# Two more units of an adjacency matrix by DMA transpose, earlier loads and shifted column sums in a two-layer graph kernel

## The chip, the cores and the metric

The kernel runs on one core of a Trainium2 chip. The time is device time in microseconds (us) of one execution; lower is better. PE is TensorE, DVE is VectorE, ACT is ScalarE, POOL is GpSimd and SP is the queue that issues the DMAs.

## What is computed

`x` is 2048x512 and `adj` is 2048x2048, a symmetric pattern of nonzeros with values that are not symmetric. All arithmetic of the reference is float32.

```python
h = jnp.maximum(_layernorm(x, axis=-1), 0.0)
# first layer: quantised features and weights, then a product with adj
weight_q = _weight_quant((weight - mean) / std, wgt_alpha, 3)
support = jnp.matmul(_act_quant(h, act_alpha, 4) / act_delta, weight_q / wgt_delta)
support = jax.nn.relu(support * act_delta * wgt_delta)
support_q = _act_quant(support, act_alpha2, 4)
x = x + jnp.matmul(adj / s, support_q / support_delta) * s * support_delta
# second layer: a normalised symmetric adjacency, and two products
h = jnp.maximum(_layernorm(x, axis=-1), 0.0)
a = (adj + adj.T) * 0.5 + jnp.eye(2048)
deg = jnp.sum(a, axis=1)
dinv = jnp.where(deg > 0, deg ** (-0.5), 0.0)
x = x + (adj @ (dinv[:, None] * a * dinv[None, :])) @ h
```

The second layer is worked as `adj @ (A @ h)`, so there are three products with a 2048x2048 matrix: the first layer's, one with the normalised symmetric matrix (called the second product below) and one with `adj` again.

## The kernel before

`adj` is cut into 32 units: unit u is the block of 128 rows number u // 2, and of these rows the columns of half u % 2 (128 x 1024 float32, 512 KB). A product with `adj` on PE needs the blocks transposed, as a pair of float16 parts (a high part, scaled by 256, and a low part that holds the rest). Both parts of all units stay in the tile `at` for the whole kernel. A unit gets there in one of two ways.

- A turned unit: PE transposes it in float32, eight blocks of 128x128 (`turn`, line 1067), ACT writes the high part from PSUM (`hi_turned`, line 514) and takes the row sum (`row_sum`, line 481), DVE takes the column sums of its eight blocks (`column_sum`, line 743) and writes the low part (`lo_turned`, line 754).
- A moved unit (the list `MOVED`): ACT writes the high part before the transpose and takes the row sum with it (`hi_rows`, line 504), DVE writes the low part (`lo_rows`, line 759), both into one of three staging places, and SP issues one DMA transpose of both parts into `at` (`move`, line 335). The k-th moved unit can be staged when the (k-3)-th has landed. PE has no work with it. For the odd units the column sums come from an accumulator that POOL adds up in float32 (line 463) and that PE turns once, as the unit called "acc". For the even moved units (`EVEN`) ACT sums the columns of the transposed unit, half a unit at a time (`sum_blocks`, line 490, four blocks each), in the places that `SUMS_OF` gives.

Each engine's order is written out by hand. PE: for each row block r from 0 to 15 `layer0(r, ...)` (line 1083), 32 matmuls of 128x512 that add up the first layer's product in PSUM; ahead of it, or in gaps of it, the turns in `TURNS[r]`. `layer0(r)` needs unit 2r at its start and unit 2r+1 at its second chunk, and, since PSUM has two banks for it, the features of block r-2 out of the bank: it waits for `x1_ready` at r-1, which `x1_tile(r - 2)` on DVE signals.

DVE (loop of line 945): in stage r, `x1_tile(r - 1)` (line 876: one SCALAR_TENSOR_TENSOR of line 882, then the statistics of lines 884 and 885), the turned unit of the stage, `lo_rows` of the units in `MOVES[r]`, the columns of units 0 and 2 (`column_sum_late`, line 749), and in four stages a part of the second product's preparation: `sum_unit(v)` (line 921) adds both parts of `at` across to a fresh copy of `adj`, `sum_lo(v)` (line 936) splits off the low part of that sum. ACT has `sum_hi(v)` (line 579) between the two.

SP (line 312): loads (`rows`, `rows_again`) and transposes (`move`) stand in one order in one queue, and a load into a used slot waits until the unit before it is done. `LOADS` says which loads follow which move. POOL adds unit u of the odd ones when it has arrived and `layer0` of an early enough block is done (`ADD_AT`).

The loop of DVE's stages, in which the order matters:

```python
for r in range(1, 14):
    x1_tile(r - 1)
    ...
    for u in moves[1:]:
        lo_rows(u)
    if r - 3 in LATE_SUMS:
        column_sum_late(r - 3)
    ...
    if r == 10:
        sum_unit(1)
```

Of the kernel before, what the change touches and what calls it, by code (L numbers as in the profile page):

```python
# [9 lines left out]
T = N // P  # L10
KD = D // P
W = N // 2
B = W // P
# [4 lines left out]
AHEAD = 20  # L18
# [8 lines left out]
EVEN = (10, 12, 14, 18, 20, 22, 26)  # L27
# [6 lines left out]
def gnn_kernel(nc, x, adj, adj_scale, weight, wgt_alpha, act_alpha, act_alpha2, out):  # L34
# [5 lines left out]
    with ctx:  # L40
# [242 lines left out]
        for u in EVEN:  # L283
# [6 lines left out]
        MOVES = {1: [9], 2: [10, 11], 3: [12], 4: [13, 14], 5: [15], 6: [17, 18], 7: [19, 20], 8: [21, 22],  # L290
                 9: [23, 25], 10: [26], 11: [27, 29]}
# [5 lines left out]
        SUMS_OF = {5: [[(10, FIRST)], [], [(10, LAST)]], 7: [[(12, FIRST)], [(12, LAST)], []],  # L297
                   8: [[(14, FIRST)], [(14, LAST)], []], 9: [[(18, FIRST)], [(18, LAST)], []],
                   10: [[], [], [(20, FIRST)]], 11: [[], [(20, LAST)], [(22, FIRST)]],
                   12: [[], [], [(22, LAST), (26, FIRST)]], 13: [[], [], [(26, LAST)]]}  # L300
# [12 lines left out]
        def _(sp):  # L313
# [47 lines left out]
            for u in range(2, 12):  # L361
# [6 lines left out]
            move(3)  # L368
            move(5)
            sp.wait_ge(sq_ready, T // 2)  # L370
            rows(14)
            rows(15)
            move(7)
            LOADS = {9: [16], 10: [17], 11: [18], 12: [19], 13: [20], 14: [21], 15: [22], 17: [23], 20: [24], 21: [25], 22: [26],
                     23: [27], 25: [29, 28], 26: [30], 27: [31]}
            for r in range(1, 12):
                for u in MOVES[r]:
                    move(u)
                    for w in LOADS.get(u, []):
                        if w < AHEAD:  # L380
                            rows(w)
                        else:
                            rows_again(w)
# [82 lines left out]
        def _(act):  # L466
# [156 lines left out]
            for r in range(1, 14):  # L623
                moves = MOVES.get(r, [])
                ahead, between, behind = SUMS_OF.get(r, [[], [], []])
                for u in TURNS[r][:1]:
                    turn_hi(u)
                for u, blocks in ahead:
                    sum_blocks(u, blocks)
                for u in moves[:1]:  # L630
                    hi_rows(u)
                for u in TURNS[r][:1]:
                    sum_rows(u)
                for u in TURNS[r][1:]:
                    turn_hi(u)
                    sum_rows(u)
                for u, blocks in between:
                    sum_blocks(u, blocks)
                for u in moves[1:]:
                    hi_rows(u)  # L640
                for u, blocks in behind:
                    sum_blocks(u, blocks)
                if r == 9:
                    sum_hi(0)
                if r == 11:
                    sum_hi(1)
# [22 lines left out]
        def _(dve):  # L669
# [275 lines left out]
            for r in range(1, 14):  # L945
# [11 lines left out]
                if r - 3 in LATE_SUMS:  # L957
                    column_sum_late(r - 3)
                if r == 8:
                    sum_unit(0)  # L960
                if r == 9:
                    sum_lo(0)
                if r == 10:
                    sum_unit(1)
                if r == 11:
                    sum_lo(1)

            a, b = LATE_SUMS[0] * B, (LATE_SUMS[-1] + 1) * B
            link(nc.vector.memset(pause[:, :], 0.0))
            link(nc.vector.tensor_scalar(colp[:, a:b], colp[:, a:b], 1.0 / SA, None, ALU.mult))  # L970
# [5 lines left out]
            for moved_sums in (rs3[:, ADDED[1] // 2:ADDED[-1] // 2 + 1, 1],  # L976
                               rs3[:, 5:14:2, 0], rs3[:, 6:11:4, 0]):
                last = nc.vector.tensor_scalar(moved_sums, moved_sums, 1.0 / SA, None, ALU.mult)
# [268 lines left out]
```

## Time and profile before

| | before |
|---|---|
| median of 3 runs | 494.21 us |
| lowest and highest | 493.84 and 494.96 us |
| the profiled execution | 493.84 us |
| its span in the trace | 492.0 us |
| PE busy | 97% of the span |
| DVE busy | 55% |
| ACT busy | 31% |
| POOL busy | 10% |

The span is the time between the first and the last instruction of the trace; some 1.8 us of the execution's time lie around it. Start times below count from the span's start. The stages r = 1 to 13 of the first product run from 45 to 143 us, `layer0(14)` and `layer0(15)` to 157 us, the second product to 323 us, and the third to the end. The number behind a waiting instruction, in square brackets, is how long its engine was idle ahead of it and what ended that.

### The profile page before, as it was taken

How to read it: one execution, taken by the hardware profiler on the slowest of the kernel's cores; microseconds unless marked ns; L12 is line 12 of the kernel's file. 1: busy time of each engine (PE TensorE's matmuls, PEld its weight loads, DVE VectorE, ACT ScalarE, POOL GpSimd, SP SyncE). 2: the span in 40 equal slices, each digit the busy share in tenths (PEclk: the TensorE clock that was granted, in tenths of full speed). 3: DMA queues.
4: the chain of work that ended last, by engine and by line, in shares of the span. 5: the costliest groups of instructions: out<-in, count | busy, mean ns of one | idle time of the engine just before them, and what ended most of it. 6: DMA issues, size and time to landing. Idle time of an engine off the chain costs nothing.

```text
span 492.0 us, 6358 instructions
## 1 busy us (share of the span) xinstructions
PE 478.2 (97%) x2358; PEld 232.0 (47%) x2358; DVE 268.4 (55%) x360; ACT 154.5 (31%) x300; POOL 47.3 (10%) x54
## 2 busy tenths in 40 slices
PE   2899999999999999999999999999999999999997
PEld 2655444444544444444444444444444444444446
DVE  5967997779998788876997777240100001000010
ACT  1887834867651354353521211230000000000000
POOL 2321953223100000000000000000000000000000
PEclk9999999999999999999999999999999999999999
DMA  8986999999794332323232321054000000100001
GB/s 303 403 319 161 224 218 248 215 233 255 178 302 191 89 126 87 125 87 99 85 117 93 121 85 43 0 183 180 36 29 21 21 21 21 43 21 21 21 23 43
DMA packets 62507, 62.65 MB, mean 127 GB/s; under 512 B 45464, under 2 KB 45720, under 8 KB 62488
## 3 DMA queue, kind: packets, MB, share of 16 engines
q1 hardware_dynamic: 62480, 62.40, 43.5%
q8 instruction: 11, 0.18, 0.1%
q14 instruction: 8, 0.07, 0.1%
q10 hardware_dynamic: 8, 0.00, 0.0%
HBM read 42.99 MB, written 8.39 MB: 104 GB/s over the span
## 4 chain that ended last, share of the span: by engine, by line
PE 92%; DVE 3%; DMA 2%; ACT 1%; SPq 1%; issue 1%; POOL 0%; ACTq 0%
PE ps_a L1202 32%; PE ps_p L1100 20%; PE ps_p L1165 8%; PE ps_a L1165 7%; PE ps_b L1165 7%; PE ps_h L1165 4%; PE ps_m L1165 4%; DMA feat<-in_x 2%; PE ps_b L1051 1%; PE ps_h L1100 1%; PE ps_m L1100 1%; DVE small L942 1%; PE ps_b L1218 1%; PE ps_a L1218 1%; PE ps_a L1051 1%; PE ps_a L1079 1%
## 5 line engine op out<-in xcount | busy, mean ns | idle before, releaser
L1100 PE MATMUL ps_p<-small,at 128*128 128x512 f16 x448 | 99.1, 379 | 0.0
L1020 DVE SCALAR_TENSOR_TENSOR feat<-ps_a,feat 128x512 f32<-128x512 f32 (+1 forms) x16 | 10.8, 675 | 148.7 <-PE ps_a L1202 144.2
L1202 PE MATMUL ps_a<-small,at 128*128 128x512 f16 x360 | 80.1, 379 | 0.0
L1202 PE MATMUL ps_a<-a_in,at 128*128 128x512 f16 x360 | 80.1, 379 | 0.0
L1100 PEld LDWEIGHTS ps_p<-small,at 128*128 128x128 f16 x448 | 43.7, 98 | 50.2
L585 ACT ACTIVATE split<-a_in 128x1024 f16<-128x1024 f32 x30 | 31.7, 1057 | 101.8 <-PE ps_p L1165 90.0
L938 DVE TENSOR_TENSOR split<-a_in,split 128x1024 f16<-128x1024 f32 x30 | 36.7, 1224 | 34.1 <-ACT split L585 34.1
L1202 PEld LDWEIGHTS ps_a<-small,at 128*128 (+1 forms) x360 | 35.2, 98 | 42.5
L1202 PEld LDWEIGHTS ps_a<-a_in,at 128*128 (+1 forms) x360 | 35.2, 98 | 42.5
L1165 PE MATMUL ps_p<-feat,split 128*128 (+1 forms) x180 | 43.9, 379 | 0.5 <-DVE small L942 0.5
L1165 PE MATMUL ps_a<-feat,split 128*128 (+1 forms) x180 | 43.8, 379 | 0.0
L1165 PE MATMUL ps_b<-feat,split 128*128 (+1 forms) x180 | 43.8, 379 | 0.0
L929 DVE TENSOR_TENSOR a_in<-a_in,at 128x1024 f32<-128x1024 f32 x30 | 36.7, 1225 | 1.0
L928 DVE SCALAR_TENSOR_TENSOR a_in<-a_in,at 128x1024 f32<-128x1024 f32 x30 | 36.5, 1217 | 0.0
L1165 PEld LDWEIGHTS ps_p<-feat,split 128*128 128x128 f16 x180 | 17.5, 98 | 22.0 <-DVE small L942 1.0
L1165 PEld LDWEIGHTS ps_a<-feat,split 128*128 128x128 f16 x180 | 17.6, 98 | 21.4 <-issue 0.5
L1165 PEld LDWEIGHTS ps_b<-feat,split 128*128 128x128 f16 x180 | 17.6, 98 | 21.2
L1165 PE MATMUL ps_h<-feat,split 128*128 (+1 forms) x90 | 24.3, 379 | 0.0
L1165 PE MATMUL ps_m<-feat,split 128*128 (+1 forms) x90 | 24.3, 379 | 0.0
L463 POOL TENSOR_TENSOR at<-at 128x1024 f32<-128x1024 f32 x8 | 21.4, 2672 | 12.6 <-PE ps_p L1100 11.8
L761 DVE SCALAR_TENSOR_TENSOR at<-at 128x1024 f16<-128x1024 f32 x12 | 18.9, 1599 | 0.0
L463 POOL TENSOR_TENSOR at<-at,a_in 128x1024 f32<-128x1024 f32 x6 | 15.9, 2654 | 26.8 <-DMA a_in<-in_adj 16.7
(182 smaller groups left out, 436.2 us busy)
## 6 DMA issues: line engine op xcount, KB each, us to landing
a_in<-in_adj SPq DMA_DIRECT2D x46, 512.0 KB, 3.9
at<-in_adj SPq DMA_DIRECT2D x16, 512.0 KB, 8.6
out<-feat SPq DMA_DIRECT2D x31, 256.0 KB, 4.2
feat<-in_x SPq DMA_DIRECT2D x8, 512.0 KB, 11.1
feat<-out SPq DMA_DIRECT2D x4, 1024.0 KB, 9.4
at<-in_L_gnn_weight SPq DMA_DIRECT2D x2, 512.0 KB, 3.9
split<-in_adj SPq DMA_DIRECT2D x1, 512.0 KB, 16.3
tmp<-in_adj SPq DMA_DIRECT2D x1, 512.0 KB, 16.4
```

What stands on the lines that cost most here:

```text
L463: nc.gpsimd.tensor_tensor(acc, acc, unit_in(u), ALU.add).then_inc(acc_done, 1)
L585: nc.scalar.activation(part(v % 2, 0), sum_in(v), ACT.Copy).then_inc(shi, 1)
L761: nc.vector.scalar_tensor_tensor(stage(u, 1), unit_in(u), SA, stage(u, 0), ALU.mult, ALU.subtract)\
L928: link(nc.vector.scalar_tensor_tensor(u3, u3, SA, at_across(h, 0, j), ALU.mult, ALU.add))
L929: last = nc.vector.tensor_tensor(u3, u3, at_across(h, 1, j), ALU.add)
L938: nc.vector.tensor_tensor(part(v % 2, 1), sum_in(v), part(v % 2, 0), ALU.subtract).then_inc(slo, 1)
L1020: nc.vector.scalar_tensor_tensor(out, products, 1.0 / (SA * SZ), out, ALU.mult, ALU.add).then_inc(y_out, 1)
L1051: last = nc.tensor.matmul(sup_banks(m)[:, t * D:(t + 1) * D], hT[m % 2][:, (t * KD + k) * P:(t * KD + k + 1) * P], w_int[:, k * D:(k + 1) ...
L1100: last = nc.tensor.matmul(l0_bank(r), at_block(r, lo, j), small[:, j * D:(j + 1) * D], start=(j == 0 and lo == 0), stop=(j == T - 1 and lo ...
L1165: last = nc.tensor.matmul(BANK[t], part(k, lo)[:, t * P:(t + 1) * P], g_part(j, g_lo), start=(first and lo + g_lo == 0), stop=False)
L1202: last = nc.tensor.matmul(BANK[n], at_block(t, lo, j), z_part(j, z_lo), start=(j == 0 and lo + z_lo == 0), stop=(j == T - 1 and lo == 1))
L1218: last = nc.tensor.matmul(BANK[1 + h][:, 0:DH], at_block(T - 1, lo, j), z_part(j, z_lo)[:, h * DH:(h + 1) * DH], start=(j == 0 and lo + z_ ...
```

## The change

Units 16 and 24 join `EVEN`, so they are moved and no longer turned; there are then 23 moved units and 9 turned ones. SP issues the loads of units 14 to 19 together, between the moves of 3 and 5 and behind a wait for the first layer's features, where two of them stood after the move of 5 and four stood after the moves of 9 to 12. The columns of 10, 14 and 18 are summed on DVE by `column_sum_late`, in stages 5, 7 and 9, and no longer on ACT; ACT's other sums have new places. `sum_unit(1)` goes from DVE's stage 10 to the end of stage 9, `sum_lo(1)` from stage 11 to stage 10, and ACT's `sum_hi(0)` and `sum_hi(1)` stand ahead of `hi_rows` in stages 9 and 10, where they stood at the ends of stages 9 and 11.

```diff
@@ -24,7 +24,8 @@
 GROUPS = (0, 2, 4, 8, 12, T)
 LATE_GROUPS = (0, 13, T)
 LATE_SUMS = (0, 2)
-EVEN = (10, 12, 14, 18, 20, 22, 26)
+EVEN = (10, 12, 14, 16, 18, 20, 22, 24, 26)
+SUMMED_LATE = (10, 14, 18)
 MOVED = tuple(sorted(tuple(range(3, 30, 2)) + EVEN))
 ADDED = tuple(range(1, 30, 2))
 TURNED = tuple(u for u in range(UNITS) if u not in MOVED)
@@ -287,17 +288,16 @@
         ROW_SUMS = {2: [0], 4: [1, 2, 4], "acc": []}
 
 
-        MOVES = {1: [9], 2: [10, 11], 3: [12], 4: [13, 14], 5: [15], 6: [17, 18], 7: [19, 20], 8: [21, 22],
-                 9: [23, 25], 10: [26], 11: [27, 29]}
+        MOVES = {1: [9], 2: [10, 11], 3: [12], 4: [13, 14], 5: [15, 16], 6: [17, 18], 7: [19, 20], 8: [21, 22],
+                 9: [23, 24, 25], 10: [26], 11: [27, 29]}
         ADD_AT = {u: (u - 7) // 2 for u in ADDED if u >= 9}
 
 
 
         FIRST, LAST = range(0, B // 2), range(B // 2, B)
-        SUMS_OF = {5: [[(10, FIRST)], [], [(10, LAST)]], 7: [[(12, FIRST)], [(12, LAST)], []],
-                   8: [[(14, FIRST)], [(14, LAST)], []], 9: [[(18, FIRST)], [(18, LAST)], []],
-                   10: [[], [], [(20, FIRST)]], 11: [[], [(20, LAST)], [(22, FIRST)]],
-                   12: [[], [], [(22, LAST), (26, FIRST)]], 13: [[], [], [(26, LAST)]]}
+        SUMS_OF = {6: [[(12, FIRST)], [(12, LAST)], []], 8: [[(16, FIRST)], [(16, LAST)], []],
+                   10: [[(20, FIRST)], [], [(20, LAST), (22, FIRST)]], 11: [[(22, LAST)], [], [(24, FIRST)]],
+                   12: [[], [], [(24, LAST), (26, FIRST)]], 13: [[], [], [(26, LAST)]]}
         PARTS = sum(len(place) for places in SUMS_OF.values() for place in places)
 
         def wait_moved(engine, u):
@@ -366,21 +366,18 @@
             rows(12)
             rows(13)
             move(3)
+            sp.wait_ge(sq_ready, T // 2)
+            for u in range(14, AHEAD):
+                rows(u)
             move(5)
-            sp.wait_ge(sq_ready, T // 2)
-            rows(14)
-            rows(15)
             move(7)
-            LOADS = {9: [16], 10: [17], 11: [18], 12: [19], 13: [20], 14: [21], 15: [22], 17: [23], 20: [24], 21: [25], 22: [26],
-                     23: [27], 25: [29, 28], 26: [30], 27: [31]}
+            LOADS = {13: [20], 14: [21], 15: [22], 16: [23], 20: [24], 21: [25], 22: [26], 23: [27], 24: [28], 25: [29],
+                     26: [30], 27: [31]}
             for r in range(1, 12):
                 for u in MOVES[r]:
                     move(u)
                     for w in LOADS.get(u, []):
-                        if w < AHEAD:
-                            rows(w)
-                        else:
-                            rows_again(w)
+                        rows_again(w)
             for v in range(2, 6):
                 free_slot(UNITS - 6 + v)
                 sums(v)
@@ -627,6 +624,8 @@
                     turn_hi(u)
                 for u, blocks in ahead:
                     sum_blocks(u, blocks)
+                if r in (9, 10):
+                    sum_hi(r - 9)
                 for u in moves[:1]:
                     hi_rows(u)
                 for u in TURNS[r][:1]:
@@ -640,10 +639,6 @@
                     hi_rows(u)
                 for u, blocks in behind:
                     sum_blocks(u, blocks)
-                if r == 9:
-                    sum_hi(0)
-                if r == 11:
-                    sum_hi(1)
 
             late_sqrt(0)
             g_tile(0)
@@ -956,17 +951,22 @@
                     lo_rows(u)
                 if r - 3 in LATE_SUMS:
                     column_sum_late(r - 3)
+                for k, u in enumerate(SUMMED_LATE):
+                    if r == (5, 7, 9)[k]:
+                        wait_moved(dve, u)
+                        column_sum_late(u)
                 if r == 8:
                     sum_unit(0)
                 if r == 9:
                     sum_lo(0)
+                    sum_unit(1)
                 if r == 10:
-                    sum_unit(1)
-                if r == 11:
                     sum_lo(1)
 
             a, b = LATE_SUMS[0] * B, (LATE_SUMS[-1] + 1) * B
             link(nc.vector.memset(pause[:, :], 0.0))
+            late_sums = colp[:, :].rearrange("p (u b) -> p u b", b=B)[:, SUMMED_LATE[0]:SUMMED_LATE[-1] + 1:4, :]
+            nc.vector.tensor_scalar(late_sums, late_sums, 1.0 / SA, None, ALU.mult)
             link(nc.vector.tensor_scalar(colp[:, a:b], colp[:, a:b], 1.0 / SA, None, ALU.mult))
             dve.wait_ge(blocks_summed, PARTS)
             nc.vector.tensor_reduce(cols[:, :], colp[:, :].rearrange("p (r t) -> p t r", t=T), AXIS.X, ALU.add)
@@ -974,7 +974,7 @@
             dve.wait_ge(rs_done, len(TURNED))
             dve.wait_ge(hi_ready, len(MOVED))
             for moved_sums in (rs3[:, ADDED[1] // 2:ADDED[-1] // 2 + 1, 1],
-                               rs3[:, 5:14:2, 0], rs3[:, 6:11:4, 0]):
+                               rs3[:, EVEN[0] // 2:EVEN[-1] // 2 + 1, 0]):
                 last = nc.vector.tensor_scalar(moved_sums, moved_sums, 1.0 / SA, None, ALU.mult)
             link(last)
             link(nc.vector.tensor_tensor(nt2[:, 0:T], rs3[:, :, 0], rs3[:, :, 1], ALU.add))
```

## Rows read from the trace of the kernel before

**Rows 1.** Windows: stretch, busy us of PE, PEld, DVE, ACT, POOL, granted clock, DMA share.

```profile
103.00:110.00 7.00, 7.00 (x34) 3.17 (x33) 4.22 (x8) 3.07 (x13) 1.16 (x1) 1.00 1.14 242
110.00:127.00 17.00, 17.00 (x89) 8.73 (x87) 16.80 (x15) 12.69 (x36) 7.70 (x3) 1.00 0.99 246
127.00:143.00 16.00, 15.97 (x87) 8.57 (x86) 15.64 (x24) 10.62 (x33) 0.00 (x0) 1.00 0.87 205
```

**Rows 2.** Chain that ended last, 80 to 158 us: start, us, what.

```profile
82.39 0.87 PE ps_a L1079 x8
...
110.89 0.87 PE ps_b L1079 x8
111.77 13.81 PE ps_p L1100 x64
125.58 0.87 PE ps_a L1079 x8
```

**Rows 3.** Timeline of DVE, stages 7 and 8: start, us, engine, line, operation.

```profile
94.48 1.23 DVE L761 SCALAR_TENSOR_TENSOR at<-a_in,at 128x1024 f16<-128x1024 f32 x1 [0.73 <-ACT at L511]
97.12 0.75 DVE L882 SCALAR_TENSOR_TENSOR feat<-ps_p,cst,feat 128x512 f32<-128x512 f32 x1 [1.42 <-PE ps_p L1100]
...
98.73 3.15 DVE L761 SCALAR_TENSOR_TENSOR at<-a_in,at 128x1024 f16<-128x1024 f32 x2
101.80 1.22 DVE L928 SCALAR_TENSOR_TENSOR split<-split,at 128x1024 f32<-128x1024 f32 x1
...
104.53 0.74 DVE L882 SCALAR_TENSOR_TENSOR feat<-ps_p,cst,feat 128x512 f32<-128x512 f32 x1
```

**Rows 4.** Timeline of DVE, stages 9 to 11.

```profile
109.97 2.30 DVE L761 SCALAR_TENSOR_TENSOR at<-a_in,at 128x1024 f16<-128x1024 f32 x1 [2.65 <-ACT at L511]
...
113.33 0.74 DVE L882 SCALAR_TENSOR_TENSOR feat<-ps_p,cst,feat 128x512 f32<-128x512 f32 x1
...
118.30 3.37 DVE L928 SCALAR_TENSOR_TENSOR tmp<-tmp,at 128x1024 f32<-128x1024 f32 x1
...
122.97 2.32 DVE L933 SCALAR_TENSOR_TENSOR tmp<-ident,tmp 128x128 f32<-128x128 f16 x1
125.22 0.74 DVE L882 SCALAR_TENSOR_TENSOR feat<-ps_p,cst,feat 128x512 f32<-128x512 f32 x1
```

**Rows 5.** Line 752, column sums of a moved unit: duration min/median/max in ns.

```profile
L752 DVE TENSOR_REDUCE colp<-at x2: 2272/2272/2273, 67.1 to 79.0; 128x8 f32<-128x2048 f16 x2
```

**Rows 6.** Timeline of POOL, additions of units 23, 25 and 27.

```profile
97.22 2.35 POOL L463 TENSOR_TENSOR at<-at,a_in 128x1024 f32<-128x1024 f32 x1 [4.55 <-PE ps_p L1100]
108.84 2.35 POOL L463 TENSOR_TENSOR at<-at,a_in 128x1024 f32<-128x1024 f32 x1 [9.27 <-DMA a_in<-in_adj]
117.35 3.25 POOL L463 TENSOR_TENSOR at<-at,a_in 128x1024 f32<-128x1024 f32 x1 [6.16 <-DMA a_in<-in_adj]
```

**Rows 7.** Timeline of ACT, `hi_rows(25)` and `sum_hi(0)`.

```profile
108.79 1.06 ACT L511 ACTIVATE at<-a_in 128x1024 f16<-128x1024 f32 x1 [3.93 <-DMA a_in<-in_adj]
...
109.85 1.04 ACT L585 ACTIVATE split<-split 128x1024 f16<-128x1024 f32 x1
```

**Rows 8.** SP: the transpose of unit 22, and line 341's landings.

```profile
104.86 3.69 SPq L341 DMA_TRANSPOSE at<-at  x1
...
DMA to landing us min/median/max: 4.2/5.6/7.1
```

**Rows 9.** Timeline of PE near its start.

```profile
10.33 1.97 PE L1079 MATMUL ps_p<-ident,a_in 128*128 128x128 f32 x8
12.25 1.75 PE L1079 MATMUL ps_a<-ident,a_in 128*128 128x128 f32 x8
13.84 0.61 PE L1041 MATMUL ps_b<-mean_of 128*128 128x128 f32 x4
...
19.67 1.89 PE L1051 MATMUL ps_b<-at 128*128 128x512 f16 x8 [1.60 <-DVE at L729]
```

**Rows 10.** Window of the loads at the start, columns as in rows 1.

```profile
12.00:40.00 28.00, 25.93 (x183) 16.34 (x182) 21.54 (x56) 22.97 (x32) 6.49 (x25) 1.00 0.90 344
```

## The prediction

> **What bounds the kernel now.** I read the windows first. In each of the three stretches between 103 and 143 us TensorE is busy throughout, at a granted clock of 1.00 [rows 1]. So in the first product nothing but TensorE's own work sets the end, and a turn taken out of it shortens the kernel by the turn's length, as long as nobody comes late. The same windows name the engine that could: VectorE is busy for 16.80 of 17 us and 15.64 of 16 us from 110 to 143 us, and it gets more work just ahead of that stretch and in it. The chain of waits says the same from TensorE's side: it is matmuls and turns without a piece of another engine, and it gives the date of each stage [rows 2]. I then read VectorE's timeline in the order of its program, because the change puts four operations into that program ahead of an operation for which TensorE waits [rows 3, 4].
>
> The cover that matters is this one. `layer0(11)` starts in the middle of the 13.81 us piece at 111.77, so at 118.7 us [rows 2]. It waits for `x1_ready` at 10, which `x1_tile(9)` gives; that stood at 113.33 and took 0.74 us [rows 4], so it was done at 114.1, 4.6 us early. `layer0(12)` waits in the same way for `x1_tile(10)`, at 125.22 and done at 125.96 [rows 4]; its start is behind the turn at 125.58 that takes 0.87 us, 126.45 [rows 2]. There the cover was only 0.5 us, because `sum_unit(1)` lay ahead of it and was held up.
>
> **The change part by part.** *The two turns.* Those at 82.39 and 110.89 take 0.87 us each [rows 2]. Both lie on the path: -1.74 us. From 83 us on each stage starts 0.87 us earlier, from 111 us on 1.74 us earlier, so `layer0(11)` wants to start at 118.7 - 1.74 = 116.9 us.
>
> *VectorE up to stage 8.* The operations have these prices. A `lo_rows` takes 1.13 us from start to start where nothing holds it (1.23 alone, at 94.48), an `x1_tile` 1.61 us (97.12 to 98.73), `sum_unit(0)` 2.73 us (101.80 to 104.53) [rows 3]. A `column_sum_late` takes 2.27 us by the two that exist, 2.20 from start to start [rows 5]. `lo_rows(20)` waited for ACT, and ACT for the landing of 17, the third moved unit before it; this is so after the change too, so I leave it at 94.5, done at 95.7. Then comes the new sum of unit 14's columns, to 97.9. `layer0(7)` is over at 96.2 by then, so `x1_tile(7)` starts 1.7 us late, at 97.9, and goes on to 99.5. `lo_rows(21)` and `lo_rows(22)` took 3.07 us together because of POOL's addition at 97.22 [rows 3, 6]; that addition comes 0.87 us earlier and falls beside the column sum, which has one operand in SBUF and wasn't lengthened by additions beside it [rows 5]. So 2.3 us, to 101.8; `sum_unit(0)` to 104.5; `x1_tile(8)` to 106.1.
>
> *VectorE in stage 9.* Here the work is three `lo_rows` where there were two, the columns of 18 (new), `sum_lo(0)` and `sum_unit(1)` (from stage 10). ACT first makes `sum_hi(0)`, 1.04 us [rows 7], which now waits for `sum_unit(0)` at 104.5 and stands ahead of `hi_rows(23)`; so 23 is staged at 106.7 and 24 at 107.8, and the `lo_rows` of both are done by about 109.1. Unit 25 is staged when the third moved unit before it has landed. That was 21; it is now 22, because 24 is in the list. The transpose of 22 was issued at 104.86, and line 341's median from issue to landing is 5.6 us [rows 8]: 110.5. SP has one transpose more and four loads fewer between 57 and 104 us; the loads were in the queue beside the transposes, and I take 22's landing as unchanged. `hi_rows(25)` ran at 108.79 [rows 7]; it now runs at 110.5, to 111.6, and `lo_rows(25)` ends at about 112.8. To this come the columns of 18, 2.2 us, to 115.0; `sum_lo(0)`, 1.13 us (109.97 plus 2.30 to 113.33 less the overlap), to 116.1; and `sum_unit(1)`, 2.73 us.
>
> *POOL in it.* In the trace, an operation of VectorE with two operands in SBUF doesn't run beside an addition of POOL: it ends some 1.08 us after the addition's end. The one at 109.97 took 2.30 us (addition over at 111.19), the one at 118.30 took 3.37 (addition over at 120.60), the one at 122.97 took 2.32 instead of some 0.3 [rows 4, 6]. The addition of 27 starts when its load lands, 117.35. The new `sum_unit(1)` runs from 116.1, so it meets that addition: 3.37 - 1.22 = 2.15 us more [rows 3, 4]. 116.1 + 2.73 + 2.15 = 121.0. Then `x1_tile(9)`, 0.74 us and a little: 121.8.
>
> *The new stall.* `layer0(11)` waits from 116.9 to 121.8: +4.9 us. Its ends: without the collision and with unit 22 landing 1 us earlier it is 1.7 us; with 25's addition (108.84) getting ahead of `lo_rows(24)`, and 22 landing 1.5 us later (the greatest of line 341 is 7.1), about 7 us [rows 6, 8]. I take the walk's value.
>
> *TensorE's clock.* At its first steady work, from 10.33 us, eight turns took 1.92 us and the next eight 1.59 (12.25 to 13.84), against 0.87 for eight later [rows 2, 9]: that is the level of 1.2 GHz first and 2.4 GHz after. Before it TensorE had been nearly idle. The sixteen cost 3.51 - 1.74 = 1.77 us more than at full speed. A gap of 1.60 us before 19.67 was followed by full speed: eight matmuls of 512 columns took 1.89 us [rows 9]. The stall here is three times as long as that gap. No row shows one of its length inside the kernel; bounds are 0, as after the gap of 1.60 us, and 1.77 us, as at the start, or somewhat above. I take 1.77, because 4.9 us without a matmul is nearer to the start's idleness.
>
> The Trainium skill, TensorE: Matmul & The Clock Gate, Part 1, says that an engine that has been idle is put back to half speed and has to earn the full one by work. By that rule the stall costs its own length and a slow start behind it; without the rule the sum would be 1.77 us smaller.
>
> *After the stall* nothing is late again by this reckoning. VectorE has less to do in stages 10 to 13 (no turn of 24, `sum_unit(1)` gone), so `x1_tile(10)` is due about 126.3 us, before `layer0(12)` at 129.6, and the statistics behind the last turn keep their distance, since the turn itself is what they wait for.
>
> *The loads of 14 to 19.* Six transfers of 0.52 MB at the 344 GB/s of the stretch at the start [rows 10] take 9.2 us. From 42.6 us (the features' end), with some 2 us until the first bytes, they end near 54 us; the transpose of 5 stands behind them and needs about 2 us more: near 56. TensorE needs it at 56.5. This cover is thin (0.5 us); a burst slower by a tenth would put a first stall of 0.5 us there. I cost it at nothing, and take 0 to 2 us for the range.
>
> *ACT and the rest.* ACT loses six half sums and two turned units with their row sums and gains four half sums and two `hi_rows`; none of it is late for TensorE. The two late scalings on VectorE cost some 0.2 us behind the last turn, with more than 8 us between them and the start of the second product, whose length is not touched.
>
> **The sum.** -1.74 + 4.9 + 1.77 = +4.9 us. Against the profiled execution that is 493.84 + 4.9 = 498.8 us with a span of about 497.0; the median of the runs lies 0.4 us above that execution, so I predict 499.1 us.
>
> **The rivals.** *Cover holds.* Should VectorE reach `x1_tile(9)` by 116.9 us, only the turns count: 494.2 - 1.7 = 492.5 us, faster. For it: VectorE had idle gaps of 2.65 and 1.42 us in stages 7 to 9 that can take work up [rows 3, 4]. Against it: the gap of 2.65 us was a wait for unit 25's load, and the later landing of 22 now fills it; 6.9 us of work stand between `lo_rows(25)` and `x1_tile(9)`'s end, so 25 would have to be staged 5 us before 22 can land. *A small stall.* If VectorE meets no addition and the transposes run 1 us ahead, the stall is 1.7 us, too short to move the clock: 494.2 us. *The clock holds.* The stall is 4.9 us and TensorE goes on at full speed: 497.3 us. *A long stall.* The transposes of 16 and 24 push the whole chain of landings back by 2 us, the additions of 25 and 27 both meet VectorE, and the turn of unit 5's data is late: stall 8 to 9 us in all, 503 us. *The slower side as one mechanism* is thus `sum_unit(1)` in front of `x1_tile(9)`: its place is the end of stage 9, its price 2.73 to 4.9 us, and it decides as soon as `lo_rows(25)` ends after 116.9 - 6.9 = 110.0 us.
>
> **How the numbers follow.** Forecast (stall of about 5 us and a slow start behind it) 0.44; the clock holds 0.26; a long stall 0.13; a small stall 0.07; cover holds 0.10. Within 0.2%, about what a measurement of this kernel can tell from no change, is within 1.0 us. The small stall gives 0.06 to no change; the rest of it and the three stalls are slower, 0.84; faster 0.10. The range leaves out the cover that holds, most of the small stalls and the longest stalls: 495.2 to 504.5 us.
>
> **What would show it.** Right: the waits of TensorE list line 1100 behind VectorE's line 882 once, 4 to 6 us, near 117 us; VectorE's timeline has line 752 at about 113 us, and one operation of line 928 or 929 of some 3.4 us near 118 us; the eight matmuls behind the stall take twice their usual time. Line 1079 has 16 matmuls fewer. Wrong: no wait of TensorE in the first product (then unit 25 was staged early, and the landing of 22 is what I misjudged), a wait that ends with a transpose's landing near 56 us, or full clock after the stall.

## The result, and the profile after

| | before | after |
|---|---|---|
| median | 494.12 us (6 runs) | 503.07 us (6 runs) |
| lowest and highest | 492.97 and 495.52 | 502.41 and 505.23 |
| the profiled execution | 493.84 us | 503.08 us |
| its span | 492.0 us | 501.3 us |

The ratio is 1.0187, with a 95% interval from 1.0167 to 1.0206: the change costs 8.95 us by the medians. The forecast was 4.9 us.

TensorE's waits in the changed kernel (waiting engine, what it works on and its line, whom it waited for; then us in total, times, longest) have one new line. Lines of this kernel are numbered a few lower than before; 1100 is the matmul of `layer0` in both, and 877 is the first operation of `x1_tile` (882 before).

```profile
PE ps_p L1100 <- DVE feat L877: 8.2, 1, 8.2
```

It lies ahead of `layer0(11)`, for `x1_tile(9)`, where the prediction put it, and is 8.2 us long instead of 4.9. Windows around it (the stretch, its length, then busy us of TensorE, its weight loads, VectorE, ScalarE, GpSimd, the granted clock, DMA share, GB/s):

```profile
117.70:126.20 8.50, 0.31 (x2) 0.00 (x0) 8.40 (x6) 0.66 (x1) 2.50 (x1) 0.81 0.96 216
126.20:129.70 3.50, 3.47 (x9) 1.27 (x10) 2.90 (x4) 3.13 (x12) 0.00 (x0) 0.50 0.97 259
129.70:135.00 5.30, 5.30 (x27) 2.48 (x26) 2.70 (x5) 5.21 (x19) 2.35 (x1) 0.99 0.93 208
```

TensorE has 0.31 us of work in the 8.5 us up to 126.2, and the granted clock falls within them (0.81 is a mean over the stretch). Behind the wait it is 0.50, the level of 1.2 GHz, while TensorE is busy; from 129.7 on it is 2.4 GHz again. The chain that ended last (start, us, what) has the price of that:

```profile
89.68 7.68 DMA at<-at
...
126.23 8.81 PE ps_p L1100 x32
135.04 0.87 PE ps_a L1079 x8
```

The 32 matmuls of `layer0(11)` take 8.81 us, against 6.91 for a stage at full speed: +1.9 us. The first row is the transpose of unit 17, 7.68 us from issue to landing.

VectorE from stage 7 to stage 10; compare [rows 3, 4]:

```profile
98.62 2.25 DVE L756 SCALAR_TENSOR_TENSOR at<-a_in,at 128x1024 f16<-128x1024 f32 x1 [4.66 <-ACT at L508]
100.80 2.27 DVE L747 TENSOR_REDUCE colp<-at 128x8 f32<-128x2048 f16 x1
102.99 0.73 DVE L877 SCALAR_TENSOR_TENSOR feat<-ps_p,cst,feat 128x512 f32<-128x512 f32 x1
...
106.83 1.22 DVE L923 SCALAR_TENSOR_TENSOR split<-split,at 128x1024 f32<-128x1024 f32 x1
...
111.80 5.65 DVE L756 SCALAR_TENSOR_TENSOR at<-a_in,at 128x1024 f16<-128x1024 f32 x3 [0.56 <-ACT at L508]
117.37 2.27 DVE L747 TENSOR_REDUCE colp<-at 128x8 f32<-128x2048 f16 x1
119.56 1.21 DVE L933 TENSOR_TENSOR split<-split 128x1024 f16<-128x1024 f32 x1
120.70 1.21 DVE L923 SCALAR_TENSOR_TENSOR tmp<-tmp,at 128x1024 f32<-128x1024 f32 x1
121.94 3.25 DVE L924 TENSOR_TENSOR tmp<-tmp,at 128x1024 f32<-128x1024 f32 x1
...
125.43 0.74 DVE L877 SCALAR_TENSOR_TENSOR feat<-ps_p,cst,feat 128x512 f32<-128x512 f32 x1
```

Line 756 is `lo_rows`, 747 `column_sum_late`, 923, 924 and 928 `sum_unit`, 933 `sum_lo`. From 98.62 to 126.2 it idles once, for 0.56 us. In the order of the program: `lo_rows(20)`, the columns of 14, `x1_tile(7)`, two `lo_rows`, the first unit's sum from 106.83, `x1_tile(8)`, three `lo_rows` in 5.65 us, the columns of 18, `sum_lo(0)`, `sum_unit(1)` and at last `x1_tile(9)` at 125.43.

GpSimd's additions of 23, 25 and 27 (answering to [rows 6]), and ScalarE's `hi_rows(20)` and `sum_hi(0)` (the second answers to one of [rows 7]):

```profile
97.43 2.36 POOL L460 TENSOR_TENSOR at<-at,a_in 128x1024 f32<-128x1024 f32 x1 [4.55 <-PE ps_p L1100]
112.78 2.44 POOL L460 TENSOR_TENSOR at<-at,a_in 128x1024 f32<-128x1024 f32 x1 [13.00 <-DMA a_in<-in_adj]
121.61 2.50 POOL L460 TENSOR_TENSOR at<-at,a_in 128x1024 f32<-128x1024 f32 x1 [6.38 <-DMA a_in<-in_adj]
```

```profile
97.44 1.06 ACT L508 ACTIVATE at<-a_in 128x1024 f16<-128x1024 f32 x1 [5.19 <-DMA at<-at]
...
109.67 1.06 ACT L582 ACTIVATE split<-split 128x1024 f16<-128x1024 f32 x1 [5.81 <-DVE split L928]
```

The addition at 97.43 is over at 99.79, and `lo_rows(20)`, begun at 98.62, ends 1.08 us behind it. The one at 112.78 holds up one of the three `lo_rows`, the one at 121.61 the second half of `sum_unit(1)` (3.25 us instead of 1.23). `hi_rows(20)` waited for the landing of 17 until 97.44.

The account of the two profiled executions: two turns -1.74, the wait 8.2, the slow stage +1.9, a wait of 0.2 us ahead of the turn of 30 gone, and the first stage began 1.1 us later than in the profile of before. That is +9.3 us, as between the spans. Of the 1.9 us, 0.2 come behind a wait at full clock too: there (unit 16 alone, below) the 32 matmuls took 7.08 us. The late start comes from the weights' statistics (TensorE waited 4.1 us for them and not 2.3). In the profiles of the twelve experiments, which begin in the same way, that wait was 2.0 to 3.5 us, so I take the late start for scatter and for no part of the change.

### The profile page after: what moved, and what is told of

The parts are those of the page before. It is cut to its first block, busy times and chain, and to the rows that moved or that the text cites. A ratio compares the mean times of both kernels' runs of the same rounds, so it can differ in the third digit from the quotient of the medians.

```text
span 501.3 us, 6306 instructions
## 1 busy us (share of the span) xinstructions
PE 478.9 (96%) x2342; PEld 231.5 (46%) x2342; DVE 271.8 (54%) x361; ACT 149.7 (30%) x282; POOL 45.8 (9%) x54
## 4 chain that ended last, share of the span: by engine, by line
PE 82%; DVE 10%; DMA 5%; ACT 1%; issue 1%; SPq 1%; POOL 0%; ACTq 0%
PE ps_a L1202 31%; PE ps_p L1100 11%; PE ps_p L1165 7%; PE ps_a L1165 7%; PE ps_b L1165 7%; PE ps_m L1165 4%; PE ps_h L1165 4%; DVE at L756 3%; DMA at<-at 2%; DMA feat<-in_x 2%; DVE colp L747 2%; PE ps_b L1051 1%; PE ps_m L1100 1%; PE ps_h L1100 1%; DVE small L937 1%; PE ps_b L1218 1%
## 5 line engine op out<-in xcount | busy, mean ns | idle before, releaser
L1100 PE MATMUL ps_p<-small,at 128*128 128x512 f16 x448 | 100.7, 384 | 8.2 <-DVE feat L877 8.2
L508 ACT ACTIVATE at<-at 128x1024 f16<-128x1024 f32 x13 | 13.7, 1055 | 19.6 <-DMA at<-at 19.6
```

Source lines behind the costliest of these rows:

```text
L508: nc.scalar.activation(stage(u, 0), unit_in(u), ACT.Copy, scale=SA, accum_out=rowsum[:, u:u + 1])\
L1100: last = nc.tensor.matmul(l0_bank(r), at_block(r, lo, j), small[:, j * D:(j + 1) * D], start=(j == 0 and lo == 0), stop=(j == T - 1 and lo ...
```

## Experiments

All ratios are to the kernel before on the same chip. Its medians were 494.1 to 494.6 us on the chips used, so a few tenths between the times of two experiments mean nothing. In what follows "the wait" is TensorE's wait ahead of `layer0(11)`; it is 8.2 us in the changed kernel.

### The second unit's sum back in stage 10

```diff
                 if r == 9:
                     sum_lo(0)
-                    sum_unit(1)
                 if r == 10:
+                    sum_unit(1)
+                if r == 11:
                     sum_lo(1)
...
-                if r in (9, 10):
-                    sum_hi(r - 9)
...
+                if r == 9:
+                    sum_hi(0)
+                if r == 11:
+                    sum_hi(1)
```

> The changed kernel with one part undone: the second product's second unit is summed in stage 10 and split in stage 11, as before, and ScalarE's parts of it stand at the ends of stages 9 and 11. Theory (VectorE's order: whatever stands ahead of x1_tile(9) delays layer0(11) by its own length): the sum took 4.7 us there, from 120.7 to 125.4, so TensorE's wait ahead of layer0(11) falls from 8.2 to about 3.5 us, a wait that may still lower the clock; time about 498.4 us, or 496.5 if the clock holds. Rival 1 (pace of the transposes: units 16 and 24 make every landing late): the wait stays at 7 us or more, time about 502 us. Rival 2 (VectorE's load as such, not its order): what is gained at layer0(11) is lost at layer0(12), which waits for x1_tile(10): waits sum to 8 us again, time about 503 us.

499.92 us, ratio 1.0095 (1.0069 to 1.0121); the profiled execution is the slowest of five, 502.63 us.

```profile
PE ps_p L1103 <- DVE feat L879: 3.6, 1, 3.6
...
PE ps_p L1103 <- DMA at<-at: 2.4, 1, 2.4
PE ps_b L1082 <- POOL at L460: 1.2, 1, 1.2
```

The wait is 3.6 us, as expected for the order of VectorE's program (3.5). It is not lost again at `layer0(12)`. But 3 us are gained and not 4.7, and two waits are new. One of 2.4 us lies near 55 us: `layer0(2)` waits for the transpose of unit 5, which stands behind the six early loads. The changed kernel's own profile doesn't show it, because there the stages began 1.1 us later. The clock fell twice, behind the wait of 2.4 us and with that of 3.6 us. In the changed kernel's five executions without a profile the mean granted clock is 0.990 and not 0.993, so this early wait may be in them; no trace shows it. The other new wait, 1.2 us, is the accumulator's turn waiting for GpSimd's addition of unit 29.

### The columns of 10, 14 and 18 back on ScalarE

```diff
-        SUMS_OF = {6: [[(12, FIRST)], [(12, LAST)], []], 8: ...
+        SUMS_OF = {5: [[(10, FIRST)], [], [(10, LAST)]], 6: [[(12, FIRST)], [(12, LAST)], []],
+                   7: [[(14, FIRST)], [(14, LAST)], []], 8: [[(16, FIRST)], [(16, LAST)], []],
+                   9: [[(18, FIRST)], [(18, LAST)], []], 10: ...
...
-                for k, u in enumerate(SUMMED_LATE):
-                    if r == (5, 7, 9)[k]:
-                        wait_moved(dve, u)
-                        column_sum_late(u)
...
```

> The changed kernel with one part undone: the columns of units 10, 14 and 18 are summed on ScalarE as before; the second product's second unit is still summed in stage 9. Theory (VectorE's work ahead of x1_tile(9)): the columns of 14 and 18, 2.2 us each, stand behind the point from which VectorE no longer idles, so the wait ahead of layer0(11) falls by 4.4 us to about 3.8 us, and the time to about 498.7 us, or 496.8 if the clock holds. The columns of 10 should be worth nothing. Rival 1 (pace of the transposes): no change, 503 us. A reckoning with the shares of the trace before the change gave a wait of only 0.8 us here, since the additions of GpSimd would then be met in another order.

498.87 us, ratio 1.0102 (1.0057 to 1.0147).

```profile
PE ps_p L1096 <- DVE feat L879: 3.9, 1, 3.9
```

3.9 us, against 3.8 expected: the columns of 14 and 18 cost their full 4.4 us in that place. My other reckoning, a wait of 0.8 us, was wrong.

### TensorE kept busy during the wait

```diff
+                    if r == 11:
+                        pe.wait_ge(atlo, turn_no(8) + 1)
+                        for _ in range(30):
+                            nc.tensor.matmul(ps_b[:, 0:D], at_block(0, 0, 0), small[:, 0:D], start=True, stop=True)
                     if 2 <= r < 14:
                         pe.wait_ge(x1_ready, r - 1)
```

> The changed kernel with 30 matmuls of 128x512 into an unused PSUM bank between layer0(10) and the wait ahead of layer0(11), some 6.5 us of work in a wait of 8.2 us; their results are read by nobody. Theory (the clock's fall is a cost of its own behind the wait): granted clock 1.00 throughout, layer0(11) takes 6.91 us and not 8.81, and the time falls by 1.9 us to about 501.2 us. Rival (the slow stretch is hidden, since VectorE is what TensorE would wait for next anyway): the clock holds but the time stays at 503 us, with a new wait of 1.9 us ahead of layer0(12) or of the turn of 30.

502.13 us, ratio 1.0146 (1.0111 to 1.0181). TensorE's waits, and windows as above:

```profile
PE ps_p L1104 <- DVE feat L877: 2.0, 1, 2.0
PE ps_p L1104 <- DMA at<-at: 1.6, 1, 1.6
...
118.00:126.00 8.00, 6.09 (x29) 2.55 (x26) 7.93 (x6) 0.63 (x1) 2.64 (x1) 1.00 1.06 228
126.00:129.60 3.60, 3.55 (x9) 1.33 (x10) 2.98 (x4) 3.23 (x12) 0.00 (x0) 0.53 1.01 262
129.60:135.00 5.40, 5.40 (x28) 2.64 (x27) 2.79 (x5) 5.31 (x21) 2.35 (x1) 1.00 1.03 200
```

The wait left over is 2.0 us, and in the profiled execution the clock still fell behind it: `layer0(11)` took 8.77 us there. In the three executions that were only timed the mean granted clock is 1.00, and they took 500.95, 501.4 and 503.56 us. By the medians the gain is 0.9 us and not 1.9, and the intervals of the two kernels overlap. So the price of the slow stage rests on the rows of the changed kernel (8.81 against 6.91 us); that filling the wait brings it back was not shown.

### GpSimd's additions made small

```diff
-                    nc.gpsimd.tensor_tensor(acc, acc, unit_in(u), ALU.add)
+                    nc.gpsimd.tensor_tensor(acc[:, 0:16], acc[:, 0:16], unit_in(u)[:, 0:16], ALU.add)
```

> The changed kernel, but GpSimd adds 16 of the 1024 columns of each odd unit: most of its additions are left out, and with them its hold on what VectorE reads. Theory (operations of VectorE with two operands in SBUF stand still beside an addition): the three meetings ahead of x1_tile(9), 1.1 us at 98.6, 2.3 us in the three lo_rows at 111.8 and 2.1 us in the second unit's sum at 121.9, are gone; the wait ahead of layer0(11) falls by 5.5 us to 2.7 us, and the time to about 497.6 us, or 495.7 if the clock holds. Rival (the long durations come from memory traffic of the transposes): the long operations stay, 503 us.

This kernel leaves out most of the column sums of the odd units. 500.34 us, ratio 1.0121 (1.0093 to 1.015). TensorE's wait, then VectorE's `lo_rows(20)`, `lo_rows(23)` with `lo_rows(24)`, and the second half of `sum_unit(1)`:

```profile
PE ps_p L1100 <- DVE feat L877: 3.8, 1, 3.8
...
96.96 1.23 DVE L756 SCALAR_TENSOR_TENSOR at<-a_in,at 128x1024 f16<-128x1024 f32 x1 [4.16 <-ACT at L508]
...
109.11 2.36 DVE L756 SCALAR_TENSOR_TENSOR at<-a_in,at 128x1024 f16<-128x1024 f32 x2 [0.56 <-ACT at L508]
...
119.16 1.23 DVE L924 TENSOR_TENSOR tmp<-tmp,at 128x1024 f32<-128x1024 f32 x1
```

All long operations are short again, at the same traffic of transposes: 1.23 instead of 2.25 us, 2.36 for two, 1.23 instead of 3.25. So it is the additions that hold VectorE up. The wait fell by 4.4 us and not 5.5, because `lo_rows(25)` now waits for ScalarE (1.96 us), which waits for the landing of 22: part of what the meetings cost had been hidden behind that landing. The time was expected at 497.6 us; only the profiled execution (498.22, the fastest of four) comes near it, so its wait may be shorter than that of the others.

### Parts of the change in the kernel before

The second unit's sum early, alone (ScalarE's parts of it stand where the change puts them):

```diff
                 if r == 9:
                     sum_lo(0)
-                if r == 10:
                     sum_unit(1)
-                if r == 11:
+                if r == 10:
                     sum_lo(1)
```

> The kernel before with one part of the change alone: the second product's second unit is summed at the end of stage 9, split in stage 10, and ScalarE's parts of it stand where the change puts them. Theory (order matters only where VectorE has no idle time left ahead of x1_tile(9)): x1_tile(9) was done 4.6 us ahead of layer0(11); the sum takes 2.7 us, or 4.9 us beside an addition of GpSimd, so there is no wait at layer0(11), or one below 0.5 us, and the tight place ahead of layer0(12) gets looser: 494.3 us, no change. Rival (this part alone carries the loss): a wait of 3 us or more ahead of layer0(11), 498 us.

493.9 us, ratio 0.9989 (0.9977 to 1.0002), with no wait of TensorE for `x1_tile`. The same edit that costs 4.7 us of the wait in the changed kernel costs nothing here, where the cover is 4.6 us.

The columns on VectorE, alone:

```diff
-        SUMS_OF = {5: [[(10, FIRST)], [], [(10, LAST)]], 7: [[(12, FIRST)], [(12, LAST)], []],
-                   8: [[(14, FIRST)], [(14, LAST)], []], 9: [[(18, FIRST)], [(18, LAST)], []],
+        SUMS_OF = {7: [[(12, FIRST)], [(12, LAST)], []],
...
+                for k, u in enumerate(SUMMED_LATE):
+                    if r == (5, 7, 9)[k]:
+                        wait_moved(dve, u)
+                        column_sum_late(u)
...
```

> The kernel before with another part alone: the columns of units 10, 14 and 18 are summed on VectorE in stages 5, 7 and 9. Theory: the 2.2 us of unit 18 delay x1_tile(9) within its cover of 4.6 us, and then x1_tile(10), whose cover is 0.5 us: a wait of 0.6 to 1.7 us ahead of layer0(12) and 0.3 us ahead of the turn of 30, time 495.4 to 496.3 us. Rival (VectorE's idle time takes it up): 494.5 us.

495.13 us, ratio 1.001 (0.9997 to 1.0022).

```profile
PE ps_p L1106 <- DVE feat L882: 0.9, 1, 0.9
...
PE ps_a L1085 <- DVE at L756: 0.3, 1, 0.3
```

0.9 us ahead of `layer0(12)`, whose cover was 0.5 us, and 0.3 ahead of the turn of 30: the expected places and sizes. The time stayed 0.3 us under the expected range, and by its interval it can't be told from no change.

### The loads as before

```diff
-            sp.wait_ge(sq_ready, T // 2)
-            for u in range(14, AHEAD):
-                rows(u)
             move(5)
+            sp.wait_ge(sq_ready, T // 2)
+            rows(14)
+            rows(15)
             move(7)
-            LOADS = {13: [20], ...
+            LOADS = {9: [16], 10: [17], 11: [18], 12: [19], 13: [20], ...
...
```

> The changed kernel with one part undone: units 14 to 19 are loaded behind the same moves as before. Theory (the loads ahead of the move of 5 cost a wait of their own and give nothing back later): in the profiles of two of the experiments TensorE waited 2.4 and 1.6 us near 55 us for the transpose of unit 5, which stands behind six loads; with the old order that wait is gone, the one ahead of layer0(11) stays at 7 to 9 us, time about 501.5 us. Rival 1 (the early loads are what keeps the later transposes in time): the wait ahead of layer0(11) grows by the four loads that stand among the transposes again, 1.9 us each, to 10 us or more, time 504 us or more. Rival 2 (the loads delay all later landings): the wait falls below 6 us, time below 500 us.

502.77 us, ratio 1.0168 (1.0144 to 1.0192).

```profile
PE ps_p L1103 <- DVE feat L880: 8.2, 1, 8.2
```

The wait is again 8.2 us. The wait for unit 5 that two experiments had is not there, and the time is that of the changed kernel within 0.3 us. That a stage which TensorE begins earlier only lengthens the later wait is argued and not shown. The early loads are neither the cause of the loss nor a help.

### Without unit 16, and with one load later

The changed kernel with 16 turned again. Its sums leave ScalarE's list, and the load of 23 goes behind the move of 17, as before the change:

```diff
-EVEN = (10, 12, 14, 16, 18, 20, 22, 24, 26)
+EVEN = (10, 12, 14, 18, 20, 22, 24, 26)
...
-            LOADS = {13: [20], 14: [21], 15: [22], 16: [23], 20: [24], ...
+            LOADS = {13: [20], 14: [21], 15: [22], 17: [23], 20: [24], ...
...
```

> The changed kernel with unit 16 turned again (24 still moved, all else as changed; the load of 23 stands behind the move of 17, as before). Theory (the transpose of 16 and the load in front of the one of 17 make lo_rows(20) start 3 to 4 us late, and VectorE runs without idle time from there to x1_tile(9)): 17 lands at about 93 us again, the wait ahead of layer0(11) falls by 2.5 to 3 us to 5.5 us, and with a turn of 0.87 us more the time is about 501.2 us. Rival (the landing of 22, for which ScalarE waits in stage 9, sets the date whatever comes before): the wait stays at 7.5 us or more and the time at 503 to 504 us.

502.12 us, ratio 1.0169 (1.0144 to 1.0193); the profiled execution took 500.42 us. The wait, and `lo_rows(20)` and `lo_rows(25)` on VectorE:

```profile
PE ps_p L1100 <- DVE feat L877: 5.7, 1, 5.7
...
96.52 1.22 DVE L756 SCALAR_TENSOR_TENSOR at<-a_in,at 128x1024 f16<-128x1024 f32 x1
...
113.66 1.23 DVE L756 SCALAR_TENSOR_TENSOR at<-a_in,at 128x1024 f16<-128x1024 f32 x1 [2.63 <-ACT at L508]
```

Then the changed kernel with that load alone behind the move of 17, and 16 still moved:

```diff
-            LOADS = {13: [20], 14: [21], 15: [22], 16: [23], 20: [24], ...
+            LOADS = {13: [20], 14: [21], 15: [22], 17: [23], 20: [24], ...
```

> The changed kernel with the load of 23 behind the move of 17 and not ahead of it; nothing else is touched. Theory: as for the kernel with 16 alone, 17 lands some 1.8 us earlier and the wait ahead of layer0(11) falls from 8.2 to about 6.4 us: 501.3 us. Rival (stage 9 waits for the landing of 22 anyway, so gains ahead of it are lost): no change, 503 us.

500.89 us, ratio 1.0137 (1.0118 to 1.0156). The wait, then `lo_rows(20)`, `lo_rows(25)` and `x1_tile(9)`:

```profile
PE ps_p L1100 <- DVE feat L877: 5.5, 1, 5.5
...
95.37 1.23 DVE L756 SCALAR_TENSOR_TENSOR at<-a_in,at 128x1024 f16<-128x1024 f32 x1 [2.34 <-ACT at L508]
...
112.51 1.23 DVE L756 SCALAR_TENSOR_TENSOR at<-a_in,at 128x1024 f16<-128x1024 f32 x1 [2.63 <-ACT at L508]
...
121.72 0.74 DVE L877 SCALAR_TENSOR_TENSOR feat<-ps_p,cst,feat 128x512 f32<-128x512 f32 x1
```

In both, `lo_rows(20)` starts at 96.5 and 95.4 instead of 98.6, and the wait is 5.7 and 5.5 us instead of 8.2. One load moved by one place gives 2.2 us by the medians. In both, unit 17 lands at 94.1 us (97.36 in the changed kernel, 93.21 before). So the second shows that the load's place is enough, and no run shows that the transpose of 16 costs anything there once the load stands behind 17. Where `lo_rows(20)` is early, VectorE waits in stage 9 for ScalarE and the landing of 22 (2.63 us in both, in the brackets of the last `lo_rows` row), and the walk from there is the prediction's: 112.5 and then 1.1, 2.2, 1.1, 2.7 and 2.1, so `x1_tile(9)` starts at 121.7. The prediction had 121.0 for this start (its 121.8 is the end). In the first of the two, a wait 2.5 us shorter and one turn more should give 1.6 us. The medians give 0.95, with runs from 500.4 to 504.1 us; that difference stays open.

### Unit 16 alone, and the moves alone

Two attempts at a better kernel start from the kernel before. The first moves 16 only, keeps the sums on ScalarE (those of 16 in stage 9, the second half of 18's in stage 10), and sums the second unit in stage 9:

```diff
-EVEN = (10, 12, 14, 18, 20, 22, 26)
+EVEN = (10, 12, 14, 16, 18, 20, 22, 26)
...
-            LOADS = {... 15: [22], 17: [23], ...
+            LOADS = {... 15: [22], 16: [23], ...
...
```

> The kernel before with unit 16 moved too and 24 still turned, the columns of all even moved units on ScalarE, the loads as before, and the second product's second unit summed in stage 9. Theory (each part is free as long as VectorE reaches x1_tile(9) in time): one turn of 0.87 us is gone, VectorE has 2.2 us less of turned columns and low part and 1.1 us more of lo_rows, no new wait: 493.6 us. Rival (pace of the transposes: that of 16 alone makes 17 land 4 us later, as in all profiles of the changed kernel, where it took 7.7 us and not 5.3): lo_rows(20) comes 3 us late, the rest of stages 7 to 9 with it, and layer0(11) waits 1 to 3 us: 495 to 497 us.

495.77 us, ratio 1.003 (1.0014 to 1.0046): slower by 0.3%, with a wait, as the rival had it. The wait, `lo_rows(20)` and `lo_rows(25)`:

```profile
PE ps_p L1098 <- DVE feat L881: 1.6, 1, 1.6
...
97.45 2.34 DVE L760 SCALAR_TENSOR_TENSOR at<-a_in,at 128x1024 f16<-128x1024 f32 x1 [3.41 <-ACT at L512]
...
112.52 2.29 DVE L760 SCALAR_TENSOR_TENSOR at<-a_in,at 128x1024 f16<-128x1024 f32 x1 [2.47 <-ACT at L512]
```

The same with the load of 23 behind the move of 17:

> The kernel with unit 16 alone moved (495.8 us) and the load of 23 one move later, behind that of 17 and not ahead of it. Theory (the queue of transposes is full there, and what stands ahead of 17 delays lo_rows(20)): 17 lands some 1.8 us earlier, the wait of 1.6 us ahead of layer0(11) goes, and the time is 493.8 to 494.2 us. Rival (in stage 9 the wait for the load or landing ahead of lo_rows(25), 2.5 us, takes up whatever VectorE gains before it): the wait stays at 1.3 us or more, 495.5 us.

497.39 us, ratio 1.0064 (1.0051 to 1.0076): worse by 1.6 us, where I expected 1.6 us less.

```profile
PE ps_p L1098 <- DVE feat L881: 2.6, 1, 2.6
PE ps_b L1077 <- DMA a_in<-in_adj: 1.1, 1, 1.1
```

Unit 17 landed 0.9 us earlier (95.3 instead of 96.2), but that of 16, ahead of it, landed 2.1 us later (93.7), and `lo_rows(20)` started at 97.55, where it had started at 97.45. It met no addition, though. Behind it the later loads show: that of 25 lets `lo_rows(25)` start at 113.5 instead of 112.5, and a turn in stage 12 now waits 1.1 us for its own. That the same edit helped the changed kernel because its stages 7 and 8 had no idle time, and hurts here because waits for loads in stage 9 decide, fits these rows but was not tried.

Last, both units moved and nothing else of the change. ScalarE's sums have new places for this, and of the loads that of 28 goes behind the move of 24, that of 29 stays behind the move of 25:

```diff
-EVEN = (10, 12, 14, 18, 20, 22, 26)
+EVEN = (10, 12, 14, 16, 18, 20, 22, 24, 26)
...
```

> The kernel before with units 16 and 24 moved and nothing else of the change: the columns of all even moved units on ScalarE, the second product's second unit in stage 10, the loads as before with that of 23 behind the move of 17. Theory (the parts of the loss add up, and each that is undone gives back its length): the wait ahead of layer0(11) is gone (8.2 us less 4.7 for the second unit's sum, 2.2 or more for the columns, 1.9 for the load), and the clock holds; left is a wait of 1 to 2 us in stage 12, since the accumulator's last unit, 29, is loaded later than before; with two turns of 0.87 us fewer that gives 493.5 to 494.9 us, no change to be told from before. Rival (two transposes more are too many for the queue whatever else is done): waits of 3 us or more in stages 11 to 13, 496 us or more.

500.96 us, ratio 1.0126 (1.0103 to 1.0148). TensorE's waits, then SP's issues (the last load is that of unit 29) and GpSimd's addition of it:

```profile
PE ps_b L1081 <- POOL at L465: 4.5, 1, 4.5
...
PE ps_p L1102 <- DVE feat L884: 1.2, 1, 1.2
...
118.12 3.62 SPq L343 DMA_TRANSPOSE at<-at  x1
121.80 0.56 SPq L320 DMA_DIRECT2D a_in<-in_adj  x1
122.49 4.13 SPq L343 DMA_TRANSPOSE at<-at  x1
126.72 0.52 SPq L320 DMA_DIRECT2D a_in<-in_adj  x1
...
131.19 2.35 POOL L465 TENSOR_TENSOR at<-at,a_in 128x1024 f32<-128x1024 f32 x1 [6.37 <-DMA a_in<-in_adj]
```

The wait ahead of `layer0(11)` is down to 1.2 us, so that part of the reckoning held. But the parts don't add up to nothing: SP issues transposes and loads without a pause, unit 29 is loaded at 126.72 and added at 131.19, where before it was added at 121.9, and the accumulator's turn in stage 12 waits 4.5 us for it. What came is the rival's wait. That two transposes more are too many for that queue, whatever the order, is not shown: no run loads 29 earlier.

## Why the prediction came out as it did

Right, by the runs: the turns gone (-1.74 us, 16 matmuls of line 1079 fewer); the place of the new wait and its cause, `sum_unit(1)` and the columns ahead of `x1_tile(9)` (undoing either takes 4.6 and 4.3 us off the wait); that the additions of GpSimd lengthen VectorE's operations, and which one the addition of 27 would meet; that the clock would fall, 1.9 us against 1.77 forecast; nothing late from stage 12 on in the changed kernel. The rivals "cover holds", "a small stall" and "the clock holds" are out. The range held the time, near its upper end.

The step that failed is "`lo_rows(20)` waited for ACT, and ACT for the landing of 17 ...; this is so after the change too, so I leave it at 94.5". It waited for the same landing, but that landing moved: 97.36 instead of 93.21 us, and `lo_rows(20)` started at 98.62. TensorE's stages are 1.1 us later in this profile, so 3.0 of these 4.1 us count in the wait. They are the queue's. SP issued the transpose of 15 even earlier than before (80.81 and 81.36 us), but then it had the transpose of 16 and the load of 23 in front of that of 17, which it issued at 89.68 instead of 87.87; and 17 took 7.7 us to land instead of 5.3. The two experiments that clear that place give back 2.5 and 2.7 us of the wait, the second with the load alone.

A second premise fell with it: "I take 22's landing as unchanged". It landed at 114.54 us, where the walk had 110.5 and the kernel before 110.60. SP's queue stood idle until VectorE's late `lo_rows(21)` was done, and the transposes of 21 and 22 followed at 105.81 and 108.87, where they had been issued at 100.68 and 104.86. ScalarE's `hi_rows(25)` waited for that landing (SP's issues of 21 and 22, then `hi_rows(25)`):

```profile
105.81 1.92 SPq L341 DMA_TRANSPOSE at<-at  x1
...
108.87 3.61 SPq L341 DMA_TRANSPOSE at<-at  x1
...
114.62 1.06 ACT L508 ACTIVATE at<-a_in 128x1024 f16<-128x1024 f32 x1 [1.82 <-DMA at<-at]
```

The prediction's own steps from that landing to `x1_tile(9)` are 10.5 us long, which gives 125.0; the row says 125.43. So the form of the walk was right and its dates were not. The term of the sum that was mis-sized is the stall: 4.9 forecast, 8.2 measured. I had not asked about the landing of 17, although the walk leaves VectorE no idle time between it and the three `lo_rows` of stage 9.

That the price of the slow clock was met so closely is partly luck. It was taken from the first sixteen blocks that TensorE turned. The windows read 1.00 there, but the trace's clock record begins only at 13.65 us, near the end of them, so the level was read from their durations. And the price varies: in the six other profiles with a wait of 3.6 to 8.2 us ahead of `layer0(11)`, that stage took 8.42 to 9.58 us, 1.5 to 2.7 more than 6.91.

The long stall (chance 0.13) named the right link in "the transposes of 16 and 24 push the whole chain of landings back by 2 us" (it was 4.2 us for 17 and 3.9 for 22), and its two meetings and 503 us are what came; it should have had the larger chance. It did not name the load of 23, whose place is enough to undo the delay of 17. What I put for it as a third part, the wait for unit 5, exists (1.6 and 2.4 us in two profiles), but nothing was gained where it was gone and the later wait was there.

## What to carry to other kernels

Work that is taken off the bounding engine has to go somewhere: here 1.74 us of turns became two transposes in a queue that issued nearly without pause and 4.5 us of sums on an engine with 0.5 to 4.6 us of cover, and the sum was a loss. The sums alone cost nothing that could be told (0.999 and 1.001), the moves alone 1.3%; the sums cost their full length only where the landing ahead of them was late and the cover gone. Follow the engine's program from the last point at which it idled to the operation that the bounding engine waits for, and ask of each wait at which that walk starts whether its own date has moved. Don't add the savings of single undone parts: each wait hides the next one.

## What was new about the hardware

- Waits of TensorE of 2.4 and 3.6 us (second unit's sum in stage 10) and of 4.5 us (moves alone) were followed by work at 1.2 GHz; waits of 1.6 and 2.6 us (16 alone, and with the load later) were not. The length alone doesn't decide: a wait of 2.0 us right behind 30 filling matmuls was followed by the lower level too (0.53 from 126.0 to 129.6 us), and the kernel with the wait of 2.6 us shows a mean granted clock of 1.00 in three of its six executions and 0.997 in the other three.
- The price doesn't grow with the wait: the stage behind it took 8.42 us (wait 3.6), 9.58 (3.9), 9.21 (5.5), 8.72 (5.7) and 8.81 (8.2), against 6.91.
- Operations of VectorE with two operands in SBUF are held up by an addition of GpSimd until some 1.1 us behind its end; the column sum, with one, is not. With the load of 23 later, it ran from 96.51 us beside an addition from 96.48 to 98.83 and took 2.28 us, against 2.27 alone.
- The transpose of 17 took 7.7 us from issue to landing in the changed kernel, against 5.3 before, where the queue had been idle ahead of it. In two other kernels (16 alone with the load later, and the moves alone) it was that of 16 that took 7.6 us. All three were followed at once by another transpose, but that is not the cause by itself: 16 with the load of 23 later was followed by one as well and took 5.7 us. The cause stays open.
